# Maxima sent by half batches from ScalarE's queue, and turned scores 17 heads behind the scores, in a four-stage transformer kernel on one core

## The reference, cut to what matters

```
qkv = x @ in_proj_weight.T + in_proj_bias            # 16 heads of 8
bias = min((pos_q - pos_k) * slope[h], 8)
scores = q @ k.T * 8 ** -0.5 + bias
probs = softmax(scores)
out = probs @ v ;  return out @ out_proj_weight.T + out_proj_bias
```

## Time and profile before

| | us |
|---|---|
| median of 3 runs | 986.8 (986.79 to 990.37) |
| the profiled execution | 988.53 |
| its span in the profile | 986.5 |
| first score to last score (L1569) | 477.3 to 784.4 |
| last turned score (L1599) | 808.7 |
| PE, DVE, ACT, POOL busy in the whole span | 783.2, 549.3, 395.9, 357.9 |

### The profile page before, as it was taken

How to read it: one execution, slowest core, us unless ns; L and a number is a source line. 1 busy time by engine, 2 the same in 40 slices (tenths; PEclk the granted TensorE clock), 3 DMA queues, 4 the chain that set the end, 5 groups by cost and what they waited for, 6 DMA issues and landing times.

```text
span 986.5 us, 19021 instructions
## 1 busy us (share of the span) xinstructions
PE 783.2 (79%) x5641; PEld 564.8 (57%) x5641; DVE 549.3 (56%) x2190; ACT 395.9 (40%) x947; POOL 357.9 (36%) x543
## 2 busy tenths in 40 slices
PE   0798479999999999952489999999999982038894
PEld 0676355555666677742246676667666651028883
DVE  4688573233322332333588989898987714026672
ACT  0456121222212322210036666766676661025562
POOL 5000517777850134433222423242322102744552
PEclk9999668999999999986569999999999995559997
DMA  9970001111100132303654444444443014111110
GB/s 250 155 221 0 0 1 36 40 41 41 44 0 14 52 112 78 96 30 90 128 106 95 90 108 93 102 83 106 95 85 67 3 45 155 54 53 55 50 50 14
DMA packets 75114, 72.44 MB, mean 73 GB/s; under 512 B 8125, under 2 KB 65680, under 8 KB 72732
## 3 DMA queue, kind: packets, MB, share of 16 engines
q1 hardware_dynamic: 69436, 60.38, 27.3%
q0 software_dynamic: 5600, 11.12, 3.5%
HBM read 43.71 MB, written 27.33 MB: 72 GB/s over the span
## 4 chain that ended last, share of the span: by engine, by line
PE 52%; DVE 18%; issue 12%; DMA 5%; POOL 5%; ACT 3%; DVEq 2%; SPq 2%; POOLq 0%; ACTq 0%
PE bank L1475 10%; PE bank L1476 9%; DVE rt L1065 6%; PE bank L1498 6%; PE bank L1527 4%; PE bank L1617 3%; PE bank L1569 3%; POOL sorted_rows L766 3%; PE bank L1604 3%; PE bank L1599 2%; DMA arena<-arena 2%; SPq L548 1%; DVEq L1180 1%; PE bank L1435 1%; PE bank L1707 1%
## 5 line engine op out<-in xcount | busy, mean ns | idle before, releaser
L1065 DVE CUSTOM_DVE_ANT_0 rt<-bank,alibi 128x256 f32<-128x256 f32 x512 | 192.9, 419 | 44.4 <-PE bank L1569 37.5
L973 DVE TENSOR_TENSOR arena<-arena,bank 128x512 f32<-128x512 f32 (+1 forms) x128 | 75.0, 587 | 187.8 <-ACT arena L1253 187.8
L1280 ACT ACTIVATE arena<-bank 128x512 f32<-128x512 f32 x256 | 150.6, 598 | 55.4 <-PE bank L1604 49.5
L1253 ACT ACTIVATE arena<-bank 128x512 f32<-128x512 f32 (+1 forms) x128 | 66.1, 517 | 202.9 <-PE bank L1476 202.9
L1569 PE MATMUL bank<-arena 72*128 72x256 bf16 x512 | 104.7, 289 | 26.6 <-DMA arena<-qk_parts 13.4
L1599 PE MATMUL bank<-arena 81*128 81x256 bf16 x512 | 117.0, 274 | 8.3 <-ACT arena L1280 4.7
L1475 PE MATMUL bank<-arena 128*128 128x320 f32 (+2 forms) x256 | 115.7, 534 | 7.5 <-DVE arena L973 7.5
L1476 PE MATMUL bank<-arena 128*128 128x320 f32 (+2 forms) x256 | 111.9, 519 | 0.0
L1604 PE MATMUL bank<-arena,ident_b 128*128 128x256 bf16 (+8 forms) x544 | 80.2, 243 | 0.0
L1569 PEld LDWEIGHTS bank<-arena 72*128 72x128 bf16 x512 | 39.0, 102 | 69.4 <-DVE arena L1065 42.8
L1475 PEld LDWEIGHTS bank<-arena 128*128 128x128 f32 x256 | 42.8, 193 | 53.5 <-DVE arena L973 41.1
(11 more groups left out here) (242 smaller groups left out, 1402.9 us busy)
## 6 DMA issues: line engine op xcount, KB each, us to landing
arena<-qk_parts SPq DMA_DIRECT2D x48, 192.0 KB
arena<-qk_parts SPq DMA_DIRECT2D x144, 64.0 KB
qk_parts<-arena SPq DMA_DIRECT2D x16, 384.0 KB, 2.8
back_rows<-empty_row SPq DMA_DIRECT2D x1, 4096.0 KB, 37.8
arena<-back_rows SPq DMA_DIRECT2D x16, 256.0 KB, 3.8
arena<-in_w SPq DMA_DIRECT2D x2, 2048.0 KB, 10.9
xg_rows<-empty_row SPq DMA_DIRECT2D x1, 2580.0 KB, 38.5
arena<-xg_rows SPq DMA_DIRECT2D x8, 322.5 KB, 4.0
```

What stands on the lines that cost most here:

```text
L973: nc.vector.tensor_tensor(out, sil[:, k, 0:out.shape[1]], bank[4 + k][:, 0:out.shape[1]], ALU.mult).then_inc(hid_done, 1)
L1065: last = nc.vector.tensor_tensor_reduce(biased[n % 2 * QT + u], bank[n % 2][:, SEQ * u:SEQ * u + SEQ], alibi[:, h, P * (1 - u):P * (1 - u) ...
L1253: nc.scalar.activation(sil[:, k, 0:width], bank[2 + k][:, 0:width], ACT.Silu).then_inc(sil_done, 1)
L1280: nc.scalar.activation(prT3[:, n % (2 * HG)].rearrange("p k t -> p (k t)"), bank[2 + n % 2][:], ACT.Exp).then_inc(exp3_done, 1)
```

## The change

Three things change at once.

First, the maxima are split, turned, copied and sent for half a batch (8 heads) at a time: `max_parts_0`, `max_parts_1`, `turn_max` and `copy_max` run twice for each batch, each on 16 instead of 32 numbers a partition (24 instead of 48 partitions behind the turn). Second, the DMA is issued by ScalarE right behind its copy, and `send_max` is gone from SyncE, whose order is now `load_given(c + 4)`, `replicate(c + 2)`. Third, as eight heads are enough, EXP_LAG goes from 25 to 17, and the steps behind the turned scores come 8 to 10 slots earlier; the steps ahead of the scores are spread differently (combine in 5 and 7 of each 16 slots where it was 7 and 8, statistics 12, variance 14, norm 16), and `root5` is done one batch earlier in GpSimd's order.

```diff
-EXP_LAG = 25
-COMBINE_0, COMBINE_1, STATS, VARIANCE, NORM, TURN, HT, QKV, QK_COPY, VALUES = -41, -40, -39, -38, -33, -30, -29, -26, -25, -19
-SPLIT_MAX_0, SPLIT_MAX_1, TURN_MAX, COPY_MAX = NH + 1, NH + 2, NH + 4, NH + 5
+EXP_LAG = 17
+MH = NH // 2
+COMBINE_0, COMBINE_1, STATS, VARIANCE, NORM, TURN, HT, QKV, QK_COPY, VALUES = -43, -41, -36, -34, -32, -30, -29, -26, -25, -19
+SPLIT_MAX_0, SPLIT_MAX_1, TURN_MAX, COPY_MAX = MH + 1, MH + 2, MH + 4, MH + 5
 BACK = NH - 1 + EXP_LAG + 5
...
-NORM_5, TURN_5, COPY_5, ROUTER_5, LOGITS_5 = BACK + 22, BACK + 27, BACK + 28, BACK + 30, BACK + 31
-ROOT_LAG = 5
+NORM_5, TURN_5, COPY_5, ROUTER_5, LOGITS_5 = BACK + 22, BACK + 25, BACK + 26, BACK + 28, BACK + 29
+ROOT_LAG = 4
...
-        def send_max(c):
-
-            wait_apart(sp, (max_rows_done, c + 1))
-            sp.dma_start(qs[MROW:KALL, c % RING], max_rows[0:PARTS * NH, c % 2]).then_inc(max_in[c % 2], 16)
...
-        def max_parts_0(c):
-
-
-            wait_apart(dve, (max3_done, NH * (c + 1)), *([(max_tr, c)] if c >= 1 else []))
-            nm = nmax3[:, c % 2]
+        def max_parts_0(m):
+
+
+            wait_apart(dve, (max3_done, MH * (m + 1)), *([(max_tr, m)] if m >= 1 else []))
+            nm = nmax3[:, m // 2 % 2, :, MH * (m % 2):MH * (m % 2) + MH]
...
+        def copy_max(m):
+            act.wait_ge(max_tr, m + 1)
+            if m >= 2:
+                act.wait_ge(max_in[m % 2], 16 * (m // 2))
+            nc.scalar.activation(max_rows[0:PARTS * MH, m % 2], bank[7][0:PARTS * MH, 0:P].bitcast(BF16), ACT.Copy).then_inc(max_rows_done, 1)
+            c, h = m // 2, MH * (m % 2)
+            wait_apart(act, (max_rows_done, m + 1))
+            act.dma_start(qs[MROW:KALL, c % RING, h:h + MH], max_rows[0:PARTS * MH, m % 2]).then_inc(max_in[m % 2], 16)
...
+        def turn_max(m):
+            pe.wait_ge(max_parts_done, m + 1)
+            if m >= 1:
+                pe.wait_ge(max_rows_done, m)
+            pe.wait_ge(qk3_done, min(m // 2 + 3, BATCH))
+            if m >= 7 and m % 2 == 1:
+                pe.wait_ge(lg5_done, (m - 5) // 2)
...
-            if h == 0:
-                pe.wait_ge(max_in[c % 2], 16 * (c // 2 + 1))
+            if h % MH == 0:
+                m = n // MH
+                pe.wait_ge(max_in[m % 2], 16 * (m // 2 + 1))
```

More of the change, by code:

```diff
@@ L95, in batch_at, with half_batch_at @@
     return c if r == 0 and 0 <= c < BATCH else None
+def half_batch_at(slot, offset):
+    m, r = divmod(slot - offset, MH)
+    return m if r == 0 and 0 <= m < 2 * BATCH else None
 def head_at(slot, offset):
@@ L269, in _build @@
     nmax3 = carve([P, 2, QT, NH])
-    max_rest = carve([P, QT, NH])
-    max_part = carve([P, QT, PARTS, NH], BF16)
+    max_rest = carve([P, QT, MH])
+    max_part = carve([P, QT, PARTS, MH], BF16)
     max_rows = carve([P, 2, SEQ], BF16)
@@ L558, in _ @@
                 replicate(c + 2)
-            send_max(c)
         sp.wait_ge(st3_mm, NH * BATCH)
@@ L1060, in row_max @@
             wait_apart(dve, (s3_mm, n + 1), *([(max3_done, n - 1)] if n >= 2 else []))
-            if h == 0 and c >= 2:
-                dve.wait_ge(max_parts_done, c - 1)
+            if h % MH == 0 and c >= 2:
+                dve.wait_ge(max_parts_done, n // MH - 3)
             for u in range(QT):
@@ L1117, in _ @@
                 row_max(n)
[L1118 to L1121, removed]
+            if (m := half_batch_at(slot3, SPLIT_MAX_0)) is not None:
+                max_parts_0(m)
+            if (m := half_batch_at(slot3, SPLIT_MAX_1)) is not None:
+                max_parts_1(m)
             if (c := batch_at(slot3, COMBINE_0)) is not None:
@@ L1345, in _ @@
                 copy_qk(c)
-            if (c := batch_at(slot3, COPY_MAX)) is not None:
-                copy_max(c)
+            if (m := half_batch_at(slot3, COPY_MAX)) is not None:
+                copy_max(m)
             if (c := batch_at(slot3, COPY_OUT)) is not None:
@@ L1551, in project @@
             if c >= 3:
-                pe.wait_ge(max_rows_done, c - 2)
+                pe.wait_ge(max_rows_done, 2 * c - 4)
             for a in range(2):
@@ L1571, in score @@
             last.then_inc(s3_mm, 1)
[L1573 to L1579, removed]
+        def turn_max(m):
[5 more added lines that the diff above has]
+                pe.wait_ge(lg5_done, (m - 5) // 2)
             for u in range(QT):
-                last = nc.tensor.transpose(bank[7][0:PARTS * NH, P // 2 * u:P // 2 * u + P // 2].bitcast(BF16),
+                last = nc.tensor.transpose(bank[7][0:PARTS * MH, P // 2 * u:P // 2 * u + P // 2].bitcast(BF16),
                                            max_part[:, u].rearrange("p a h -> p (a h)"), ident_b[:])
@@ L1645, in turn5 @@
             pe.wait_ge(h5_done, e + 1)
-            pe.wait_ge(qk3_done, min(e + 7, BATCH))
-            pe.wait_ge(max_rows_done, min(e + 4, BATCH))
+            pe.wait_ge(qk3_done, min(e + 6, BATCH))
+            pe.wait_ge(max_rows_done, min(2 * e + 7, 2 * BATCH))
             if e >= 1:
@@ L1675, in _ @@
                 project(c)
-            if (c := batch_at(slot3, TURN_MAX)) is not None:
-                turn_max(c)
+            if (m := half_batch_at(slot3, TURN_MAX)) is not None:
+                turn_max(m)
             if (c := batch_at(slot3, TURN_0)) is not None:
```

13 lines of the change are left out of this document (4 added, 9 removed).

## The result

| | before | after |
| --- | --- | --- |
| median of the runs | 988.5 us (986.8 to 990.4, 4 runs) | 1005.5 us (1001.8 to 1006.5, 4 runs) |
| profiled execution, its span | 988.5, 986.5 | 1006.5, 1004.7 |
| mean granted clock | 0.906 | 0.905 |

The changed kernel is slower: ratio 1.0165, interval 1.0128 to 1.0202. Runs more than 1.5% above a kernel's fastest are left out of its ratio, which concerns `e7_front_early` alone (three of five). The changed kernel's lines there: scores L1573 (L1569 before), row maximum L1066 (L1065), turned scores L1604 (L1599), bias matmuls L1609, exponential L1281, send L1311 on ScalarE.

A forecast was written before the change was run, and what follows sets the result against it. TensorE (97% busy) and VectorE (90%) were both taken as near their limit, each waiting for the other. Terms -7.0 + 10.4 + 0 + 0 + 2 = +5.4 us on the median 986.8 gave 992.2 us, range 980 to 1004.

The forecast's parts named there:

- The lag: Eight slots leave scores alone (-9.4 us) and turned scores alone (-7.8), eight more hold both (+10.2): -7.0 us.
- The halves: Slots 1 to 8 heavy for TensorE, 9 to 16 light; period 20.5 us against 19.7, over 13 batches +10.4 us.
- about a slot's (1.1 us) can slip under TensorE's heavy half: VectorE's light-half work partly hides in slots 1 to 8, as TensorE may lead two heads; period at least 19.7 us.
- VectorE's share of the light half: Slots 9 to 16: eight row maxima, one split of two steps, division and other steps, together 9.1 us.
- Sends: Half-batch sends land within the four slots from copy to first use, 6 us heavy half, 4.6 light; cost 0.
- a rival at 1010: Sends land late: even sends miss their use by 2.2 us a batch, total 1008 to 1025 us; chance 0.13.
- in its own queue it need not stand behind them: A send in ScalarE's queue need not wait behind the replication's twelve loads in SyncE's queue; late-landing cost 0.
- ScalarE's send: Issue ahead of the next exponential, 0 to 1 us twice a batch against 32% idle; 0, other end +2 us.
- First both-slots at the low clock: First slots holding both begin eight slots earlier, at mean granted clock 0.53, with heads 0 to 3: +2 us (0 to 4).
- GpSimd: root5 one batch earlier waits for a variance, so parts come some 2 us later; nobody is near, cost 0.
- all that follows the last turned score: The chain behind the last turned score keeps its links; nothing was put there.

The follow-up runs named there:

- e7_front_early: Changed kernel, lag still 17, with the steps ahead of the scores 6 to 12 heads earlier and turn5, router and root5 back; 1.0396 times the kernel before.
- e5: Changed kernel whose replication, from batch 4 on, loads head 0's rows only; 1.0174 times the kernel before.
- e6: Changed kernel with half-batch sends issued by SyncE again, even ones between store and loads of the replication, odd ones behind the loads; 1.0148 times the kernel before.
- e1: Changed kernel, lag still 17, with norm to values (projections among them) about four heads later; 1.0705 times the kernel before.

## Why the prediction was wrong

Forecast 992.2 us, range 980 to 1004; measured 1005.5. The sign was right and the main mechanism too, the size was not.

- **The lag.** Forecast -9.4 and -7.8 for the slots that leave the two ends; measured -10.3 and -6.3. Eight more slots that hold both: forecast +10.2, and at the measured 21.16 / 16 us a slot +10.6. Together -6.0 for a forecast -7.0.
- **The halves: the step that failed.** The sums were 11.7 us of TensorE in the heavy half and 9.1 us of VectorE in the light half; measured 11.50 and 9.57. The step "about a slot's (1.1 us) can slip under TensorE's heavy half" gave the lower bound of 19.7, and so the middle of 20.5. Nothing slips in sum: TensorE's heavy half has no gap, and at its end VectorE has nothing left to do and stands 0.9 us for the first score of the light half. The period is 21.07 us, above the 20.8 without any slip. That the two banks are what forbids the slip is my reading; no run has more of them. The term was +10.4 us; with batches 2 to 13 it measured +18.9.
- **VectorE's share of the light half** was put together from row maxima and steps at their usual lengths. The two split steps beside GpSimd were in no sum (0.92 us a batch, 0.74 of it on the path). Without them the half is 8.83, below my 9.1; with them 9.57, above.
- **Sends.** Forecast 0, with a rival at 1010. The rival named the even sends; the odd ones are those amid the loads. At landings of 4.0 to 6.7 us against some 6 us of slack in the heavy half most are just in time. One wasn't, and with the low clock behind it that batch took 5.2 us more than e5's, in the profiled execution. The premise "in its own queue it need not stand behind them" failed: in its own queue a send took 4.0 to 9.6 us beside the loads and 2.0 to 2.4 without, and behind the loads in SyncE's queue (e6) it took no longer than the changed kernel's. The Trainium skill, page "DMA: Bandwidth & Descriptors", section "Queues, rings and completion order", has each DMA engine go round its queues packet by packet, by which I had seen a send in a queue of its own wait for one packet. These runs speak against that use of it, though not against the rule: the time passed before the send's first packet.
- **ScalarE's send: 0**, as forecast (e6, the same period to 0.01 us). **First both-slots at the low clock**: forecast +2. Batches 0 and 1 together measured +0.9; this holds the 10.3 us lost and the 10.6 gained by the exchange of eight slots, which leaves some 0.6. **GpSimd**: forecast 0. It costs nothing in its own steps, but its split meets VectorE's in the light half, 0.3 to 0.4 us a batch more than the same contention cost before.

The misses add up over the profiled executions. The spans differ by 18.2 us, the forecast's sum was +5.4: 12.8 us between them. Of these the lag has 1.0, the late send 5.2, the start of the stage and all that follows the last turned score -2.1, for which I had put nothing. The other 8.7 lie in the slots that hold both, period and first slots together: 21.1 us for a forecast of 12.4.

## What to carry to other kernels

Where two engines hand over to each other with two buffers between them, sum the work of each engine for every stretch that the buffers can't bridge, take the larger one there and add these up; the averages over a batch, 92% and 87% busy here, show no bound at all. Take the sum as a floor: here it fell 0.5 to 1.0 us short of a batch of 20. Don't take off what a lead between the engines might hide before a trace shows it. A shift of one pipeline stage against another is a change of that sum, and it moves transfers against each other as well: look up what lands between issue and use before and after the shift. Count the slack of a small transfer against the whole length of a large one beside it; here a queue of its own made no difference.

## What the runs showed of the hardware

- A send of 12 KB in a queue of its own landed in 2.0 to 2.4 us with the other queue quiet or lightly loaded (e5) and in 4.0 to 9.6 us beside loads of 192 and 64 KB (the changed kernel, e1). Of the one looked at, no packet moved for 4.4 us, and then all 27 in the next 1.4.
- A VectorE step of 0.17 us on operands in SBUF took up to 0.73 us beside a GpSimd operation of 1.15 us and ended with it. The row maxima, 0.42 us each, which read scores from PSUM, kept their length beside the same operations (677.86 and 678.20 us, 0.41 each).
- Behind a wait of TensorE for 2.28 us in the changed kernel's light half the granted clock was 0.50 for 10.2 us. The batch took 5.2 us more than e5's without either, so by difference the low clock cost a little more than the wait.
